# A transformer block on one core: the opening's loads and its order on the engines are changed

## Chip, cores and metric

The kernel runs on one core of a Trainium2 chip, on its five engines: TensorE (PE), VectorE (DVE), ScalarE (ACT), GpSimd (POOL) and SyncE (SP, which issues most DMAs here). The metric is the time of one execution in microseconds (us) on the device; the median of several runs counts.

## What is computed

```python
x = L0_attn_x                                   # (4, 2048, 256)
x = x + layernorm(attn(layernorm(x), Wqk, Wv, Wo, tau))
x = x + layernorm(ffn(layernorm(x), ln_g, ln_b, Wr, W1, W3, W2, W1s, W3s, W2s))

def attn(x):                                    # 16 heads of 16 channels, attention over channels
    qk = heads(x @ Wqk); v = heads(x @ Wv)
    dot = einsum('bhdn,bhen->bhde', qk, qk); q2 = sum(qk * qk, -1)
    logits = (2 * dot - q2[..., :, None] - q2[..., None, :]) / sqrt(n) * tau
    return merge(einsum('bhde,bhen->bhdn', softmax(logits), v)) @ Wo

def ffn(x):                                     # a shared expert and 2 of 7 routed ones, with capacity
    h = layernorm(x) * ln_g + ln_b
    shared = silu(h @ W1s) * (h @ W3s) @ W2s
    return routed(h) + shared
```

## The kernel before

The 8192 rows of x stand in 16 groups of 512 (four tiles of 128 rows each), four groups to a batch. Since the attention mixes channels, a batch needs only the gram matrix of its normalized x (256x256): from it come the scores, the softmax, and one matrix M (Wv, attention and Wo in one) by which all rows of the batch are multiplied. So the program opens with batch 0: load x, normalize its four groups (`x_stats`, `x_norm`), add up the gram on PE (`x_gram`), then the small steps `m_gram` to `m_low` that end in M's high and low half, then per group `o_mix` (x times M), `o_stats`, `o_norm`, `o_apply` (a layernorm, on ScalarE), `o_add` (the residual), `u_stats`, `u_norm` (the second layernorm) and `u_turn0`, `u_turn1` (transposes into h). The feed-forward part then runs in chunks of 512 rows: eight blocks m of products with W1 and W3 (`up`), silu on ScalarE, the product of the two on DVE (L1738), a high and a low half of it (`high`, `low`), and the product with W2 (`down`). Every matmul of large weights is three (`three`, L1140 to L1142): operands are split in a high part and the rest, so each weight piece is copied on ScalarE (`high_piece`, steps `w_first`) and its rest taken on DVE (`low_piece`, steps `w_first_low`); pieces 0 to 3 are W1 and W3, pieces 4 and 5 W2's halves. x transposed is split the same way, by `x_keep` on ScalarE and `x_low` on DVE.

The order is a hand-written table: `put` enters a step, with batch and group, at a place; places -56 to -1 are the opening (`BEFORE` = 56 of them), later ones lie in the chunks, two to a block. Each engine walks the places in turn and issues its own part of every step, so a step's place decides what stands before it in each engine's queue. `attend` does that; in the chunks `between(2 * m)` and `between(2 * m + 1)` call it behind the blocks' own work. `keep_clock` puts products of a matrix of ones behind some steps of the opening, into a bank that nobody reads.

SP issues DMAs in the order of its own list: two groups of x, Wv, the other two, Wqk, and so on. A step `x_stats` has a part on DVE (means and variances) and one on POOL, which raises variances to the power -0.5 (L780, L784, L788). In the first chunk PE's `up` waits for `first_lo` (h's first low half) and `w_lo` (W1's and W3's low parts). A chunk's block m waits until the silu and the product of block m - 1 have read the banks.

## Time and profile before

| | us |
|---|---|
| median of 3 runs (1087.91 to 1089.88) | 1089.29 |
| the profiled execution: its time | 1087.53 |
| its span | 1085.8 |
| PE busy in the span | 1049.2 |
| DVE busy | 656.1 |
| ScalarE busy | 503.5 |
| GpSimd busy | 390.0 |

A time of a run holds the span of the core and what lies around it (here 1.73). The page's busy times are sums over the whole span; PE's 97% is the share in which some matmul was in flight, not the share of its peak. The views that count here show single instructions by time: a row has its start, its length, engine, line and operation, and in brackets the engine's idle time before it and what ended that.

### The profile page before, as it was taken

To read this page: it belongs to the slowest core of one execution; us is meant where nothing else is said; L and a number is where in the kernel's file an instruction comes from. 1 tells how busy PE (TensorE), PEld (TensorE's weight loads), DVE (VectorE), ACT (ScalarE), POOL (GpSimd) and SP (SyncE) were. 2 spreads that over 40 slices of the span, in tenths; PEclk is the share of its full clock that TensorE was granted. 3 is DMA by queue.
4 is the path that set the end of the run, shared out by engine and by line. 5 is a ranking of instruction groups with operands and counts; after the bars stand their busy time and mean duration, and the time that the engine had idled before them with its cause. 6 is when DMAs were issued, how large, how long until landed. Compare 5 with 4: busy or idle time off the path is not lost.

```text
span 1085.8 us, 19513 instructions
## 1 busy us (share of the span) xinstructions
PE 1049.2 (97%) x6863; PEld 958.5 (88%) x6863; DVE 656.1 (60%) x1714; ACT 503.5 (46%) x895; POOL 390.0 (36%) x347
## 2 busy tenths in 40 slices
PE   7998999999999999999989999999999999999995
PEld 6886888888888988889878899999999999999874
DVE  7768864677754578754786334545545463635686
ACT  4343344443434444443454334554546463645485
POOL 3112661114640114541116731344443343312386
PEclk9999999999999999999999999999999999999998
DMA  8322460242540223461134214524344342333699
GB/s 280 114 98 78 138 214 20 78 157 93 174 142 20 100 96 141 134 221 49 59 136 162 93 43 152 139 62 117 82 96 106 68 124 52 81 79 105 239 237 178
DMA packets 47229, 129.15 MB, mean 119 GB/s; under 512 B 10276, under 2 KB 17576, under 8 KB 47152
## 3 DMA queue, kind: packets, MB, share of 16 engines
q1 hardware_dynamic: 28656, 92.83, 25.1%
q0 software_dynamic: 18496, 35.35, 14.2%
q8 instruction: 43, 0.70, 0.3%
q14 instruction: 34, 0.28, 0.1%
HBM read 73.72 MB, written 54.40 MB: 118 GB/s over the span
## 4 chain that ended last, share of the span: by engine, by line
PE 82%; DVE 8%; POOL 3%; issue 3%; ACT 1%; DMA 1%; DVEq 0%; SPq 0%; POOLq 0%; ACTq 0%
PE bank L1140 25%; PE bank L1142 25%; PE bank L1141 25%; PE bank L1159 3%; POOL out_dram L908 2%; POOL sb_place_of L913 2%; DVE sb_act L1738 1%; PE bank L1266 1%; PE bank L1319 1%; DVE sb_act_lo L1714 1%; PE bank L1219 1%; DVE sb_stX L1431 1%; DVE sb_st L1431 1%; PE bank L1278 1%; ACT sb_ln_o L967 1%
## 5 line engine op out<-in xcount | busy, mean ns | idle before, releaser
L1140 PE MATMUL bank<-sb_h_hi,sb_wup_lo 128*128 128x512 f32 (+2 forms) x960 | 354.4, 369 | 5.3 <-DVE sb_act L1738 3.8
L1738 DVE TENSOR_TENSOR sb_act<-bank,sb_act 128x512 f32<-128x512 f32 (+2 forms) x240 | 148.6, 619 | 345.9 <-PE bank L1142 317.1
L1142 PE MATMUL bank<-sb_h_hi,sb_wup_hi 128*128 128x512 f32 (+2 forms) x960 | 350.0, 365 | 0.0
L1141 PE MATMUL bank<-sb_h_lo,sb_wup_hi 128*128 128x512 f32 (+2 forms) x960 | 349.6, 364 | 0.0
L1063 ACT ACTIVATE sb_act<-bank 128x512 f32<-128x512 f32 (+2 forms) x240 | 129.8, 541 | 354.6 <-PE bank L1142 328.9
L1140 PE MATMUL bank<-sb_wdn_hi,sb_act_lo 128*128 128x256 f32 (+1 forms) x848 | 246.5, 291 | 5.8 <-DVE sb_act_lo L1714 5.8
L1142 PE MATMUL bank<-sb_wdn_hi,sb_act_hi 128*128 128x256 f32 (+1 forms) x848 | 240.1, 283 | 0.0
L1141 PE MATMUL bank<-sb_wdn_lo,sb_act_hi 128*128 128x256 f32 (+1 forms) x848 | 239.9, 283 | 0.0
L1140 PEld LDWEIGHTS bank<-sb_h_hi,sb_wup_lo 128*128 128x128 f32 x960 | 180.5, 188 | 27.2 <-DVE sb_act L1738 6.4
L1142 PEld LDWEIGHTS bank<-sb_h_hi,sb_wup_hi 128*128 128x128 f32 x960 | 180.5, 188 | 22.5
L1141 PEld LDWEIGHTS bank<-sb_h_lo,sb_wup_hi 128*128 128x128 f32 x960 | 180.9, 188 | 17.0
L1140 PEld LDWEIGHTS bank<-sb_wdn_hi,sb_act_lo 128*128 128x128 f32 (+1 forms) x848 | 159.7, 188 | 11.6 <-DVE sb_act_lo L1714 6.9
L1714 DVE TENSOR_TENSOR sb_act_lo<-sb_act,sb_act_hi 128x512 fp32r<-128x512 f32 (+2 forms) x240 | 147.2, 613 | 36.1 <-ACT sb_act_hi L1034 34.8
L1141 PEld LDWEIGHTS bank<-sb_wdn_lo,sb_act_hi 128*128 128x128 f32 (+1 forms) x848 | 159.6, 188 | 3.3
L1142 PEld LDWEIGHTS bank<-sb_wdn_hi,sb_act_hi 128*128 128x128 f32 (+1 forms) x848 | 159.5, 188 | 0.0
L1034 ACT ACTIVATE sb_act_hi<-sb_act 128x512 fp32r<-128x512 f32 (+2 forms) x240 | 136.6, 569 | 0.3 <-DVE sb_act L1738 0.3
L864 POOL DMA_INDIRECT y_scratch<-sb_ysb,sb_scur x42 | 76.9, 1832 | 154.1 <-ACT sb_ysb L1052 87.8
L784 POOL TENSOR_TENSOR sb_rstdB<-sb_veB,sb_mhalf 128x4 f32<-128x4 f32 x16 | 19.0, 1187 | 218.1 <-DVE sb_veB L1557 218.1
L800 POOL DMA_INDIRECT sent_scratch<-sb_rows,sb_sendto x64 | 70.7, 1104 | 28.9 <-issue 19.9
L833 POOL DMA_INDIRECT sb_rows<-sent_scratch,sb_gcur x42 | 44.6, 1063 | 77.3 <-issue 52.5
L788 POOL TENSOR_TENSOR sb_rstd<-sb_ve,sb_mhalf 128x4 f32<-128x4 f32 x16 | 19.8, 1239 | 77.5 <-DVE sb_ve L1593 77.5
L967 ACT ACTIVATE sb_ln_o<-bank,sb_nbiasB,sb_rstdB 128x256 f32<-128x256 f32 x64 | 30.9, 563 | 27.5 <-DVE sb_nbiasB L1562 27.5
(265 smaller groups left out, 1240.6 us busy)
## 6 DMA issues: line engine op xcount, KB each, us to landing
sb_xin<-in_L_ffn_W_dram SPq DMA_DIRECT2D x28, 512.0 KB, 3.5
sb_x<-in_L_attn_x_dram SPq DMA_DIRECT2D x16, 512.0 KB, 3.7
out_dram<-sb_x SPq DMA_DIRECT2D x16, 512.0 KB, 3.5
sb_xin<-in_L_attn_x_dram SPq DMA_DIRECT2D x14, 512.0 KB, 5.1
sb_xin<-in_x_turned_dram SPq DMA_DIRECT2D x14, 512.0 KB, 3.9
y_scratch<-sb_ysb SPq DMA_DIRECT2D x14, 512.0 KB, 3.6
sb_xn<-in_L_ffn_W_dram SPq DMA_DIRECT2D x14, 512.0 KB, 3.9
hT_scratch<-sb_hr SPq DMA_DIRECT2D x12, 512.0 KB
```

Source lines behind the costliest of these rows:

```text
L800: pool.indirect_dma_start(sent_d, bass.IndirectOffsetOnAxis(ap=sendto[:, q, t, c:c + 1], axis=0), u[q][:, t, :], None).then_inc(sent[q], 16)
L833: pool.indirect_dma_start(rows[0:w, part, t, :], None, sent_d, bass.IndirectOffsetOnAxis(ap=gcur[0:w, part, t:t + 1], axis=0)).then_inc(ga ...
L864: pool.indirect_dma_start(y_d, bass.IndirectOffsetOnAxis(ap=scur[0:w, par, part, t:t + 1], axis=0), ysb[0:w, part, t, :], None, compute_op ...
L967: ins = s.activation(ln_o[:, t, :], bank[o_bank(b, q) + t // 2][:, (t % 2) * D:(t % 2 + 1) * D], ACT.Identity, scale=rstdB[:, t:t + 1], bi ...
L1034: s.activation(act_hi[:, m % 4, 0:c.w], act[:, m % 3, 0:c.w], ACT.Copy).then_inc(ahi_ok, 1)
L1063: s.activation(act[:, m % 3, 0:c.w], a[:, 0:c.w], ACT.Silu).then_inc(silu_ok, 1)
L1140: t_.matmul(o, a_lo, b_hi, start=start, stop=False, skip_group_check=True)
L1141: t_.matmul(o, a_hi, b_lo, start=False, stop=False, skip_group_check=True)
L1142: return t_.matmul(o, a_hi, b_hi, start=False, stop=stop, skip_group_check=True)
L1159: ins = t_.matmul(bank[4 + k][:, o:c], a[:, k * P:(k + 1) * P], a[:, o:c], start=(q == 0 and t == 0), stop=(q == GB - 1 and t == GT - 1))
L1714: v.tensor_tensor(act_lo[:, m % 4, 0:c.w], act[:, m % 3, 0:c.w], act_hi[:, m % 4, 0:c.w].bitcast(F32), ALU.subtract).then_inc(alo_ok, 1)
L1738: v.tensor_tensor(act[:, m % 3, 0:c.w], bank[(4 if c.wide and m % 2 else 0) + 1][:, 0:c.w], act[:, m % 3, 0:c.w], ALU.mult).then_inc(act_o ...
```

## The change

- SP loads x's four groups first, the first in two halves of two tiles. Then it waits until the third group has landed, and goes on: x transposed (group 0), Wqk, W1's first half, x transposed (group 1), Wv (now to a place of its own, `wv`), Wo, the rest.
- In the four groups of batch 0 DVE normalizes two tiles and writes -mean/deviation (`nbX`), ScalarE normalizes the other two. POOL takes the first power ahead of three of its constants.
- PE begins with 88 products of ones. Wv's transposed product (`wv_turn`) moves from the front to two places behind the attention scores, its copy (`wv_keep`) behind the exponential. Of the ones behind `m_dots`, `m_rowdiag` and `u_turn1` (18, 40, 36), 12 stay behind the second half of `wv_turn` and 12 behind `u_turn1`.
- The table moves `x_keep`, `x_low`, `w_first`, `w_first_low` and `scale_taus`. Two of DVE's steps, W2's second low half and `x_low` of group 3, go into the first chunk.
- The first up-product of the program (`first_up`) starts from the high half of h alone and adds the products with the low half last; ScalarE writes both high halves straight from PSUM.

```diff
         X_FIRST_AT = (("x_stats", (8, 9, 11, 13)), ("x_norm", (10, 12, 14, 15)), ("x_gram", (10, 12, 14, 15)),
-                      ("x_turned", (14, 14, 14, 15)), ("x_keep", (16, 18, 24, 26)), ("x_low", (19, 20, 34, 34)))
+                      ("x_turned", (14, 14, 14, 15)), ("x_keep", (13, 18, 27, 29)), ("x_low", (17, 24, 35, BEFORE + 4)))
         M_FIRST_AT = (20, 22, 22, 23, 24, 25, 26, 28, 30, 31, 32, 33, 34, 35, 36, 36, 37)
...
-        put(0, -BEFORE, 0, [("scale_taus", 25)])
-        for j, at in enumerate((17, 19, 19, 29, 33, 34)):
+        put(0, -BEFORE, 0, [("scale_taus", 23), ("wv_keep", 33)])
+        put(0, -BEFORE, 0, [("wv_turn", 27)])
+        put(0, -BEFORE, 1, [("wv_turn", 31)])
+        for j, at in enumerate((17, 21, 26, 28, 37, 37)):
             put(0, -BEFORE, j, [("w_first", at)])
-        for j, at in enumerate((19, 24, 24, 34, 38, 38)):
+        for j, at in enumerate((19, 24, 34, 45, 49, BEFORE + 2)):
             put(0, -BEFORE, j, [("w_first_low", at)])
...
+            for landed, tiles in ((x_early, slice(0, GT // 2)), (xres_in[0], slice(GT // 2, GT))):
+                sp.dma_start(x2[:, 0, tiles, :], x_t[0][:, tiles, :]).then_inc(landed, 16)
+            sp.dma_start(x2[:, 1, :, :], x_t[1]).then_inc(xres_in[1], 16)
             for k in range(2):
-                sp.dma_start(x2[:, k, :, :], x_t[k]).then_inc(xres_in[k], 16)
+                sp.dma_start(xin[:, k, :, :], x_t[2 + k]).then_inc(x_in_s[k], 16)
...
             for k in range(2):
                 sp.sem_inc(x_in_s[k], 16)
-            weight(tsb, Wv, wv_in)
-            for k in range(2):
-                sp.dma_start(xin[:, k, :, :], x_t[2 + k]).then_inc(x_in_s[k], 16)
+            sp.wait_ge(x_in_s[0], 32)
+            sp.sem_inc(sp_go, 1)
+            turned = lambda q: sp.dma_start(turned_at(0, q).rearrange("p k n -> p (k n)"), x_turned[q]).then_inc(xT_in[q], 16)
+            turned(0)
             weight(wqk, Wqk, const_in)
             w_load(0, 0)
-            for q in range(2):
-                sp.dma_start(turned_at(0, q).rearrange("p k n -> p (k n)"), x_turned[q]).then_inc(xT_in[q], 16)
+            turned(1)
+            weight(wv, Wv, wv_in)
             weight(wo, Wo, const_in)
             for j in (1, 2):
                 w_load(0, j)
...
             made(v.affine_select(out=earlier[:, :], in_=onesb[:, :], compare_op=ALU.is_ge, fill=0.0, base=-1,
                                  pattern=[[1, P]], channel_multiplier=-1))
+            x_rstd(0, 0)
             made(v.affine_select(out=center, in_=center, compare_op=ALU.is_equal, fill=-1.0 / D, base=0,
                                  pattern=[[P, KC], [-1, D]], channel_multiplier=1))
...
+            def x_norm(b, q):
+
+                if b > 0:
+                    return
+                act_e.wait_ge(x_nb, q + 1)
+                x = x2[:, q, :, :] if q < 2 else xin[:, q % 2, :, :]
+                for t, done in ((2, xn_third), (3, xn_ok)):
+                    s.activation(xnorm[q % 2][:, t, :], x[:, t, :], ACT.Identity, scale=rstdX[:, q, t:t + 1],
+                                 bias=nbX[:, q % 2, t:t + 1]).then_inc(done, 1)
...
+            def first_keep(k):
+                act_e.wait_ge(ut_ps, OPEN + k + 1)
+                act_e.wait_ge(vec_in, 48)
+                s.activation(h_hi[:, shared_chunk(0, 0).slot, k, :], bank[6 + k][:, :], ACT.Identity,
+                             scale=gcol[:, k:k + 1], bias=bcol[:, k:k + 1]).then_inc((first_hi, hhi_ok)[k], 1)
+                if k == 1:
+                    s.activation(hfull[:, 1, :], bank[7][:, :], ACT.Identity,
+                                 scale=gcol[:, 1:2], bias=bcol[:, 1:2]).then_inc(hT_ok, 1)
+
             def u_keep(k):
                 def step(b, q):
-                    if opens(b, q) and k == 1:
+                    if opens(b, q):
+                        first_keep(k)
                         return
                     act_e.wait_ge(ut_ps, OPEN + b * (2 * GB) + (2 * q + k + 1))
                     act_e.wait_ge(lg_ps, OPEN + b * GB + q)
-                    if b == 0 and q == 0:
-                        act_e.wait_ge(vec_in, 48)
                     if q == 0:
                         act_e.wait_ge(hlo_ok, b * GB)
                     else:
                         act_e.wait_ge(h_out, OPEN + b * H_LOADS + 16 * (q - 1))
-                    if opens(b, q):
-                        s.activation(h_hi[:, shared_chunk(0, 0).slot, 0, :], bank[6][:, :], ACT.Identity,
-                                     scale=gcol[:, 0:1], bias=bcol[:, 0:1]).then_inc(first_hi, 1)
                     s.activation((hfull if q == 0 else hr)[:, k, :], bank[6 + k][:, :], ACT.Identity,
                                  scale=gcol[:, k:k + 1], bias=bcol[:, k:k + 1]).then_inc(hT_ok, 1)
                 return step
 
-            steps = {"x_high": x_high, "x_keep": x_keep, "m_gram": m_gram,
+            def wv_keep(b, q):
...
-            act_e.wait_ge(wvT_ps, 1)
-            s.activation(wvT[:, :, :].rearrange("p k d -> p (k d)"), bank[6][:, :], ACT.Copy).then_inc(wvT_ok, 1)
             steps["w_first"] = lambda b, j: high_piece(0, j, 0, stage_first)
-            def h_first(b, q):
-                slot = shared_chunk(0, 0).slot
-                act_e.wait_ge(hT_ok, OPEN + 2)
-                s.activation(h_hi[:, slot, 1, :], hfull[:, 1, :], ACT.Copy).then_inc(hhi_ok, 1)
-
             def silu_ready(b, q):
...
-                    if b == 0 and t < GT - 1:
-                        pe.wait_ge(xn_tile, q * (GT - 1) + t + 1)
+                    if b == 0 and t < GT // 2:
+                        pe.wait_ge(xn_tile, q * (GT // 2) + t + 1)
                     elif b == 0:
-                        pe.wait_ge(xn_ok, OPEN + (q + 1))
+                        pe.wait_ge((xn_third, xn_ok)[t - 2], (0, OPEN)[t - 2] + (q + 1))
...
+            def first_up(c):
+
+                pe.wait_ge(first_hi, 1)
+                pe.wait_ge(w_lo, 4)
+                for k, turned in ((0, first_hi), (1, hhi_ok)):
+                    pe.wait_ge(turned, 1)
+                    for which in range(2):
+                        for w in (wup_lo, wup_hi):
+                            t_.matmul(bank[which][:, :], w[c.wset][:, which, k, 0:P], h_hi[:, c.slot, k, :],
+                                      start=(k == 0 and w is wup_lo), stop=False, skip_group_check=True)
+                for k, rest in ((0, first_lo), (1, hlo_ok)):
+                    pe.wait_ge(rest, 1)
+                    for which, full in ((0, a_ps), (1, b_ps)):
+                        ins = t_.matmul(bank[which][:, :], wup_hi[c.wset][:, which, k, 0:P], h_lo[:, c.slot, k, :],
+                                        start=False, stop=(k == KC - 1), skip_group_check=True)
+                        if k == KC - 1:
+                            ins.then_inc(full, 1)
+
...
             def up(c, m, first_wide):
-                opening = isinstance(c.n, int) and c.n == 0 and m == 0
-                if opening:
-                    pe.wait_ge(first_lo, 1)
-                    pe.wait_ge(w_lo, 4)
-                elif m == 0:
+                if isinstance(c.n, int) and c.n == 0 and m == 0:
+                    first_up(c)
+                    return
+                if m == 0:
...
-            pe.wait_ge(const_ok, NCONST)
-            pe.wait_ge(wv_in, 16)
-            for k in range(KC):
+            ONES_MADE = 4
+            pe.wait_ge(const_ok, ONES_MADE)
+            for _ in range(88):
+                t_.matmul(bank[0][:, 0:P], onesb[:, :], onesb[:, :], start=True, stop=True)
+            def wv_turn(b, k):
+                if k == 0:
+                    pe.wait_ge(wv_in, 16)
                 for c in range(KC):
-                    ins = t_.matmul(bank[6][:, k * D:(k + 1) * D], tsb[:, c, k * P:(k + 1) * P], center[:, c, :],
+                    ins = t_.matmul(bank[1][:, k * D:(k + 1) * D], wv[:, c, k * P:(k + 1) * P], center[:, c, :],
                                     start=(c == 0), stop=(c == KC - 1))
-            ins.then_inc(wvT_ps, 1)
+                ins.then_inc(wvT_ps, 1)
+
+            steps["wv_turn"] = wv_turn
             def keep_clock(step, n):
 
                 def paced(b, q):
...
-            for name, n in (("m_times_wqk", {(0, 0): 3}), ("m_dots", {(0, 0): 18}), ("m_rowdiag", {(0, 0): 40}),
+            for name, n in (("m_times_wqk", {(0, 0): 3}), ("wv_turn", {(0, 1): 12}),
                             ("m_times_wo", {(0, 0): 3}), ("m_times_wv", {(0, 0): 6}), ("o_mix", {(0, 1): 25, (0, 2): 35}),
-                            ("u_turn1", {(0, 0): 36})):
+                            ("u_turn1", {(0, 0): 12})):
                 opening_steps[name] = keep_clock(steps[name], n)
...
-                for t in range(GT):
+                for t in range(GT if b > 0 else GT // 2):
                     ins = v.tensor_scalar(xnorm[q % 2][:, t, :], x_from(b, q)[:, t, :], mvX[:, q % 2, t, 0:1],
-                                          rstdX[:, q % 2, t:t + 1],
+                                          rstdX[:, q, t:t + 1],
                                           ALU.subtract, ALU.mult)
-                    if b == 0 and t < GT - 1:
+                    if b == 0:
                         ins.then_inc(xn_tile, 1)
-                ins.then_inc(xn_ok, 1)
+                if b == 0:
+                    v.scalar_tensor_tensor(out=nbX[:, q % 2, :], in0=mvX[:, q % 2, :, 0], scalar=-1.0,
+                                           in1=rstdX[:, q, :], op0=ALU.mult, op1=ALU.mult).then_inc(x_nb, 1)
+                else:
+                    ins.then_inc(xn_ok, 1)
...
             def first_keep(b, q):
                 if opens(b, q):
-                    dve.wait_ge(ut_ps, OPEN + 2)
+                    dve.wait_ge(first_hi, 1)
                     dve.wait_ge(vec_in, 48)
-                    v.tensor_scalar(hfull[:, 1, :], bank[7][:, :], gcol[:, 1:2], bcol[:, 1:2],
-                                    ALU.mult, ALU.add).then_inc(hT_ok, 1)
+                    v.tensor_scalar(hfull[:, 0, :], bank[6][:, :], gcol[:, 0:1], bcol[:, 0:1],
+                                    ALU.mult, ALU.add).then_inc(first_full, 1)
+                    dve.wait_ge(first_full, 1)
+                    dve.sem_inc(hT_ok, 1)
...
             def h_first(b, q):
                 slot = shared_chunk(0, 0).slot
-                dve.wait_ge(hT_ok, OPEN + 2)
                 for k, (ready, done) in enumerate(((first_hi, first_lo), (hhi_ok, hlo_ok))):
+                    if k == 1:
+                        dve.wait_ge(hT_ok, OPEN + 2)
                     dve.wait_ge(ready, 1)
                     v.tensor_tensor(h_lo[:, slot, k, :], hfull[:, k, :], h_hi[:, slot, k, :].bitcast(F32),
...
```

On DVE, between the gram and the scores, before: `sb_u` holds the gram (the copies out of the bank), `sb_wup_lo<-sb_rows` and `<-sb_ysb` are low parts of W1 and W3, `sb_second` and `sb_taus` belong to `scale_taus`, and `sb_hr<-bank,sb_headmask` is the first step of `m_pick`.

```order
L1470 TENSOR_TENSOR sb_wup_lo<-sb_act,sb_wup_hi 128x2x512 [waits xthi_ok]
L1482 COPY sb_u<-bank 128x128 [waits g_done]
L1495 COPY sb_u<-bank 128x128 [waits m_pe,m_chain]
L1695 TENSOR_TENSOR sb_wup_lo<-sb_rows,sb_wup_hi 128x1024 [waits w_hi]
L1695 TENSOR_TENSOR sb_wup_lo<-sb_ysb,sb_wup_hi 128x1024 [waits w_hi]
L1757 TENSOR_REDUCE sb_second<-sb_ident 128x16 [waits tau_in,const_ok]
L1758 TENSOR_SCALAR sb_taus<-sb_taus 128x2
```

The same place in the change (lines are those of the new file):

```order
L1536 COPY sb_u<-bank 128x128 [waits g_done]
L1549 COPY sb_u<-bank 128x128 [waits m_pe,m_chain]
L1813 TENSOR_REDUCE sb_second<-sb_ident 128x16 [waits tau_in,const_ok]
L1814 TENSOR_SCALAR sb_taus<-sb_taus 128x2
L1524 TENSOR_TENSOR sb_wup_lo<-sb_act,sb_wup_hi 128x2x512 [waits xthi_ok,tau_ok]
L1751 TENSOR_TENSOR sb_wup_lo<-sb_rows,sb_wup_hi 128x1024 [waits w_hi]
L1560 TENSOR_TENSOR sb_hr<-bank,sb_headmask 128x256 [waits m_pe,h_out,lg_ps]
```

`scale_taus`, with its wait for tau, now comes first behind the gram's copies, and `x_low` of group 1 (L1524) moved from before them to behind them.

On DVE in the first chunk, from block 1's product (`sb_act<-bank,sb_act`) to the next group's second norm, before (`sb_lg` are the router's values, `sb_st` and `sb_mv` statistics of `u_stats`):

```order
L1738 TENSOR_TENSOR sb_act<-bank,sb_act 128x512 [waits b_ps,silu_ok]
L1628 STREAM_TRANSPOSE sb_lg<-bank 128x128 [waits lg_ps]
L1714 TENSOR_TENSOR sb_act_lo<-sb_act,sb_act_hi 128x512 [waits dn_done,ahi_ok]
L1431 BN_STATS sb_st<-sb_x 128x6 [waits x2_ok]
L1431 BN_STATS sb_st<-sb_x 128x6 x3
L1435 BN_AGGR sb_mv<-sb_st 128x2 [waits u_chain]
L1435 BN_AGGR sb_mv<-sb_st 128x2 x3
L1593 TENSOR_SCALAR sb_ve<-sb_mv 128x4 [waits u_chain]
L1738 TENSOR_TENSOR sb_act<-bank,sb_act 128x512 [waits b_ps,silu_ok]
L1714 TENSOR_TENSOR sb_act_lo<-sb_act,sb_act_hi 128x512 [waits dn_done,ahi_ok]
L1608 TENSOR_SCALAR sb_rows<-sb_x,sb_mv,sb_rstd 128x256 [waits w_lo,b_rstd2]
```

And in the change:

```order
L1794 TENSOR_TENSOR sb_act<-bank,sb_act 128x512 [waits b_ps,silu_ok]
L1751 TENSOR_TENSOR sb_wdn_lo<-sb_ysb,sb_wdn_hi 128x1024 [waits w_hi]
L1684 STREAM_TRANSPOSE sb_lg<-bank 128x128 [waits lg_ps]
L1770 TENSOR_TENSOR sb_act_lo<-sb_act,sb_act_hi 128x512 [waits dn_done,ahi_ok]
L1476 BN_STATS sb_st<-sb_x 128x6 [waits x2_ok]
L1476 BN_STATS sb_st<-sb_x 128x6 x3
L1480 BN_AGGR sb_mv<-sb_st 128x2 [waits u_chain]
L1480 BN_AGGR sb_mv<-sb_st 128x2 x3
L1647 TENSOR_SCALAR sb_ve<-sb_mv 128x4 [waits u_chain]
L1794 TENSOR_TENSOR sb_act<-bank,sb_act 128x512 [waits b_ps,silu_ok]
L1524 TENSOR_TENSOR sb_wup_lo<-sb_xin,sb_wup_hi 128x2x512 [waits xthi_ok]
L1770 TENSOR_TENSOR sb_act_lo<-sb_act,sb_act_hi 128x512 [waits dn_done,ahi_ok]
```

W2's second low half (L1751) stands behind the product of block 1 and ahead of the statistics, `x_low` of group 3 (L1524) behind the product of block 2.

## Rows read from the trace of the kernel before

**Rows 1.** The page: PE's clock by fortieths of the span; the chain's shares by engine.

```profile
PEclk9999999999999999999999999999999999999998
...
PE 82%; DVE 8%; POOL 3%; issue 3%; ACT 1%; DMA 1%; DVEq 0%; SPq 0%; POOLq 0%; ACTq 0%
```

**Rows 2.** PE's waits, whole span: waiting line, engine waited for, us in total, times, longest.

```profile
PE bank L1140 <- DVE sb_act L1738: 3.8, 4, 2.8
...
PE bank L1140 <- ACT sb_act L1063: 1.3, 1, 1.3
```

**Rows 3.** PE's timeline: start, length, line, operation, count, idle before and its end.

```profile
6.64 3.75 PE L1382 MATMUL bank<-sb_ysb,sb_u 128*128 128x256 f32 x8 [6.64 <-DMA sb_u<-in_L_attn_Wv_dram]
10.19 3.89 PE L1159 MATMUL bank<-sb_xn 128*128 128x256 f32 x16
13.91 2.78 PE L1159 MATMUL bank<-sb_ln_o 128*128 128x256 f32 x16
16.53 2.78 PE L1159 MATMUL bank<-sb_xn 128*128 128x256 f32 x16
```

**Rows 4.** DVE's timeline while x is normalized.

```profile
4.50 1.40 DVE L1431 BATCH_NORM_STATS2 sb_stX<-sb_x 128x6 f32<-128x256 f32 x4 [4.50 <-DMA sb_x<-in_L_attn_x_dram]
...
8.59 1.38 DVE L1460 TENSOR_SCALAR sb_xn<-sb_x,sb_mvX,sb_rstdX 128x256 f32<-128x256 f32 x4
...
11.93 1.38 DVE L1460 TENSOR_SCALAR sb_ln_o<-sb_x,sb_mvX,sb_rstdX 128x256 f32<-128x256 f32 x4
```

**Rows 5.** DMA issues: destination, source, count, KB each, us from issue to landing.

```profile
sb_u<-in_L_attn_Wv_dram SPq DMA_DIRECT2D x1, 256.0 KB, 3.1
...
sb_taus<-in_L_attn_tau_dram SPq DMA_DIRECT2D x2, 0.1 KB, 4.5
```

**Rows 6.** POOL's timeline: the constant of ones, and the first power.

```profile
1.07 0.21 POOL L744 MEMSET sb_onesb<- 128x128 bf16 x1
...
6.71 1.03 POOL L780 TENSOR_TENSOR sb_rstdX<-sb_veX,sb_mhalf 128x4 f32<-128x4 f32 x1 [0.41 <-DVE sb_veX L1449]
```

**Rows 7.** ScalarE's timeline at the start of the first chunk.

```profile
48.51 0.78 ACT L986 ACTIVATE sb_h_hi<-bank,sb_bcol,sb_gcol 128x512 fp32r<-128x512 f32 x1 [5.88 <-PE bank L1250]
...
54.72 1.93 ACT L967 ACTIVATE sb_ln_o<-bank,sb_nbiasB,sb_rstdB 128x256 f32<-128x256 f32 x4 [1.68 <-DVE sb_nbiasB L1562]
56.53 0.61 ACT L1063 ACTIVATE sb_act<-bank 128x512 f32<-128x512 f32 x1
```

**Rows 8.** PE's timeline: the ones behind u_turn1.

```profile
48.53 2.17 PE L1390 MATMUL bank<-sb_onesb 128*128 128x128 bf16 x36
```

**Rows 9.** DVE's timeline: the first step of m_pick.

```profile
25.80 0.42 DVE L1506 TENSOR_TENSOR sb_hr<-bank,sb_headmask 128x256 f32<-128x256 f32 x1
```

**Rows 10.** SP's timeline: the issue of tau.

```profile
11.51 4.31 SPq L669 DMA_DIRECT2D sb_taus<-in_L_attn_tau_dram  x8
```

**Rows 11.** The chain that ended last, in order of time: start, length, what.

```profile
25.49 5.23 DMA sb_ysb<-in_L_ffn_W2s_dram
30.75 1.06 ACT sb_wdn_hi L1028
...
35.07 2.27 DVE sb_wdn_lo L1695 x2
```

**Rows 12.** DVE's timeline: h's low halves, and the product of block 2.

```profile
49.99 1.35 DVE L1767 TENSOR_TENSOR sb_h_lo<-sb_hfull,sb_h_hi 128x512 fp32r<-128x512 f32 x2 [0.45 <-ACT sb_hfull L988]
...
61.26 0.69 DVE L1738 TENSOR_TENSOR sb_act<-bank,sb_act 128x512 f32<-128x512 f32 x1
```

**Rows 13.** PE's timeline: block 2's start, and its wait in block 3.

```profile
57.21 0.48 PE L1140 MATMUL bank<-sb_h_hi,sb_wup_lo 128*128 128x512 f32 x1
...
62.00 0.50 PE L1140 MATMUL bank<-sb_h_hi,sb_wup_lo 128*128 128x512 f32 x1 [0.36 <-DVE sb_act L1738]
```

**Rows 14.** Stretches: length; busy (count) of PE, PEld, DVE, ACT, POOL; clock, DMA share, GB/s.

```profile
108.00:110.00 2.00, 2.00 (x6) 1.55 (x5) 1.64 (x6) 0.00 (x0) 0.00 (x0) 0.50 0.00 0
110.00:112.00 2.00, 2.00 (x13) 1.96 (x12) 2.00 (x8) 0.00 (x0) 1.48 (x2) 0.64 0.01 4
```

38 lines of the change are left out of this document (24 added, 14 removed).

## The prediction

> **What bounds the kernel now.** Times are us from the start of the span. I read the chain that ended last, PE's waits, the timelines of the opening engine by engine, and the DMA issues. In the chain PE holds 82% [rows 1]. So a change of the opening is worth as much as PE's work in the first shared chunk comes earlier, if nothing takes it back before PE runs without holes. After the opening PE waits little: behind DVE's product with the silu 3.8 in the whole run, one of them 2.8, and once 1.3 behind the silu itself [rows 2]. The opening is one chain: PE waits 6.64 for Wv, multiplies it, and the gram follows [rows 3]. A whole group of the gram takes 2.62 (13.91 to 16.53); the first takes 3.72, since PE starts at the lower of its two rates: eight matmuls 128x256 take 3.75 there, 0.47 each, and at that pace a group would take 5.6. (The clock's row of the page shows full rate from the start [rows 1]; the durations do not.) The gram ends at 21.95. DVE stands before it [rows 4]: statistics from 4.50, two groups' statistics before the first normalizing at 8.59, whose four tiles cost 1.38.
>
> After the gram come 13.2 us of small steps up to the mixing (35.1), then the mixing itself, a norm, a sum and a second norm. The last of them, u_norm, ends 47.8; from it the first chunk starts.
>
> **The gram: -2.45.** x's first two tiles are 256 KB; Wv's 256 KB landed 3.1 after issue [rows 5], so they land at 0.81 + 3.1 = 3.9, the others at 4.5 as now. DVE's statistics of group 0 end near 5.95 instead of 6.6. The power, 1.03 long [rows 6], ends at 7.0. DVE goes on with group 1 to 8.0, normalizes, and the first tile is there at 8.4. Per group DVE has 3.35 of work (8.59 to 11.93); two tiles fewer (0.65) and one small product more (0.1) make it 2.8. ScalarE's two tiles cost about 0.5 each, by o_apply's four in 1.93 [rows 7], beside other work; its queue is idle there. PE's 2.62 a group stays the bound, if the higher rate is there from the start.
>
> For that stand the 88 products of ones, from 1.4 (their constant is written at 1.28). At the full rate they take 0.06 each (36 in 2.17, [rows 8]), at the lower twice that. Before, PE ran slow from 6.64 to about 12.3 (the first group takes 1.1 longer, so 2.2 of it is slow), 5.7 in all. Released as late as that, at 7.1, the ones end at 9.4 (47 slow, 41 fast) and the gram at 9.4 + 4 x 2.62 = 19.9; released early enough, they end before the first tile, DVE is the bound up to the third group (its first tile at 13.95), and the gram ends at 19.2. I take 19.5: 2.45 earlier. The Trainium skill (TensorE: Matmul & The Clock Gate, "Part 1: The HAM clock gate") says that the low rate is the state at rest, that activity ends it, and that the moment varies from run to run. The trace agrees on the slow start; by the skill either end may come out, and the sum moves by 0.3.
>
> **From the gram to u_norm: -0.3.** Two things are put before the attention scores' first step (m_pick, 25.80 [rows 9]) on DVE. scale_taus now comes ahead of x_low(1) and W1's second low half; the queue from m_sym on is 0.5 + 1.2 + 1.2, so m_pick starts 4.05 after the gram instead of 3.85: +0.2. And scale_taus needs tau. Its eight loads went out from 11.51 in 4.31 [rows 10], the last at 15.3, and that one landed 4.5 later, at 19.8 [rows 5]. SP now waits for x's third group (landing about 7) before eight loads of about 0.5, so the last tau goes out near 17.0: landed between 20.1, if the same bytes ahead of it decide, and 21.5. DVE wants it at 19.5 + 1.15 = 20.65. So it is 0 to 0.9 late; I take +0.3, nearer the lower end, since the 4.5 was mostly queue. x_turned's last two loads go out behind tau, at 17.4, and are wanted at 23.4: hidden.
>
> W2: before, ScalarE waits for W2's second half (the chain has its DMA for 5.23 and its copy at 30.75 [rows 11]), and the copies of Wo's product, whose first bank is done at 30.9, begin at 31.8. With W2 behind m_high the first begins at once and the second when its bank is done: 0.75 gained. The load has time: ScalarE takes W2's second half about 34 and o_apply comes at 37.9. Wv's product (4 instructions of 0.24 each half) falls into PE's waits, beside m_pick and m_logits (25.80 to 28.9); its copy, 0.6 on ScalarE, lies between exp and Wo: nothing. o_stats, behind two low halves of W2 (2.27 from 35.07 [rows 11]), is then bound by the mixing itself, which ends at 37.85: 0.1. W1's last low half (1.2) before o_add ends when o_add can start: 0.05 lost. So 0.2 + 0.3 - 0.75 - 0.1 + 0.05 = -0.3.
>
> At u_norm's end the lead is 2.45 + 0.3 = 2.75. From here I give times in the frame of before; the lead is taken off at the end.
>
> **The first chunk: +1.6.** Before, the first up-product starts at 50.74, behind the ones and the first low half of h (49.99 on [rows 12]); block 0 is done at 53.65. Now PE needs only the high half (49.3, a copy of 0.78 from 48.51 [rows 7]), and its first block ends at about 52.2: 1.4 won. But block 2 waits for the silu of block 1, and that stands behind o_apply of group 1 on ScalarE: o_apply from 54.72, the silu at 56.53, PE's block 2 at 57.21 [rows 7, 13]. o_apply hangs on the statistics that DVE begins when h's two low halves are done, 1.35 from 49.99 [rows 12]. Those end no earlier now: the full halves come one after another (high 0 to 49.3, high 1 to 50.0, full 1 on ScalarE to 50.7, low 1 on DVE to 51.45). So block 2 starts at 57.4, **+0.2**; the 1.4 becomes a wait of PE.
>
> DVE gets two steps more in the chunk: W2's second low half behind the product of block 1, and x_low(3) behind that of block 2, 1.15 each (two of W2's in 2.27 [rows 11]). The product of block 2 runs at 61.26 [rows 12], and PE already waits for it, 0.36 at 62.00 [rows 13]. The low half in front moves it to 62.6: **+1.15**, all of it PE's. x_low(3) delays u_norm of group 1 and with it the transposes that PE comes to; PE, itself late, meets them 0.25 late: **+0.25**. Behind that DVE has holes, and PE runs without one to 92. SP now holds load, store and residual behind x_low(3) (about 64); the store and the residual load move some 7 and 3, and what needs them comes at 97: hidden.
>
> **Sum.** -2.45 - 0.3 + 1.6 = -1.15. The profiled execution took 1087.53 (span 1085.8); it becomes 1086.4. The three runs have their median 1.76 above it, at 1089.29; so **1088.1**, 0.1% less: within 0.2%, about what a measurement of this kernel can tell from no change.
>
> **The rivals.**
> *The first chunk costs nothing in the end (0.38).* PE waits 2.8 once more, behind DVE, at 104.87 to 107.62 [rows 2]. If that hole gives back what the first chunk lost, the lead of 2.75 stays: 1086.5, faster. For it: DVE has idle time between the chunk and that hole. Against: DVE's row of work before the hole begins at 80.88 with a product for which it waits on PE, so a late PE moves the hole with it. Were the extra steps cheaper in place, the result lies between.
>
> *PE falls back to the lower rate (0.12): slower.* Of the 58 ones behind the scores, 12 are left, and Wv's product does not fill the rest; between m_dots and Wo's product PE stands idle about 2.2 of 5 instead of 1.0, and in the first chunk twice for 1.6. After the hole of 2.75 the granted clock was 0.50 and then 0.64 [rows 14], the 1.2 GHz level, for some 3.4; that costs 2 x 0.5 + 2 x 0.36 = 1.7. In the opening the low rate could last as long as the first time, 5.6, over Wo's and Wv's products and the mixing: 2.8. Both: -1.15 + 2.8 + 1.7 = +3.35, 1092.6. It decides from the point where one such gap counts as rest; against it, the hole of 1.3 [rows 2] left the rate alone. The Trainium skill (same page, "HAM oscillation — how this bites in real kernels") says that pauses between bursts bring the low rate back, to be paid each time; the hole at 107 agrees, and by it this rival would have both falls.
>
> *tau comes at its latest (0.08).* +0.6 on top, 1088.7: still within 0.2%.
>
> **How the numbers follow.** The forecast alone has 0.42. Within 0.2%: 0.42 + 0.08 = 0.50; faster 0.38; slower 0.12. The lower end: gram at 19.2, tau in time, no cost in the first chunk, 2.75 + 0.3 + 0.3 = 3.35 under the median, and 0.95 for the runs' own spread (1087.91 to 1089.88): 1085.0. The upper: gram at 19.9, tau at its latest, -1.15 + 0.4 + 0.6 = -0.15, one fall of the clock of 1.7, and 0.15 for the rounding of the steps: 1091.0. The likeliest case alone spans 1086.9 to 1089.3.
>
> **What would show it.** Right: gram's end at 19.2 to 19.9; m_pick 4 behind it; no W2 on ScalarE before Wo's copies; PE's first up-block 1.4 earlier after u_norm, then a wait for a silu before block 2 and one of about 1.5 for block 2's product. Wrong: matmuls of ones at twice their length up to the gram, any slow stretch between 22 and 70, DVE waiting for tau's DMA by over 1, or a lead at 110 as large as at u_norm.

## The result and the profile after

The change makes the kernel slower: 1089.63 us (median of 20 runs, 1088.10 to 1094.04) against 1087.18 for the kernel before (20 runs, 1084.92 to 1091.51). The ratio on record is 1.0026, 95% interval 1.0015 to 1.0036 (it comes from all the runs, here and below, and so is not quite the quotient of the medians). The forecast was a gain of 1.15 us. One execution of chunk_free, a kernel further down, took 1709.58 at a granted clock of 0.56; it is left out of that kernel's ratio. The profiled execution took 1089.85 (span 1088.1), the one of before 1087.53 (1085.8): 2.3 more.

PE's timeline after the change, in the opening and in the first chunk, answers to [rows 3, 13] (start, length, line, operation, count, idle before and what ended it):

```profile
1.33 6.37 PE L1420 MATMUL bank<-sb_onesb 128*128 128x128 bf16 x88 [1.33 <-POOL sb_onesb L760]
10.19 4.53 PE L1183 MATMUL bank<-sb_xn 128*128 128x256 f32 x16 [2.49 <-DVE sb_xn L1510]
14.55 2.78 PE L1183 MATMUL bank<-sb_ln_o 128*128 128x256 f32 x16
...
19.80 2.78 PE L1183 MATMUL bank<-sb_ln_o 128*128 128x256 f32 x16
...
47.98 0.61 PE L1271 MATMUL bank<-sb_ident,sb_u 128*128 128x128 f32 x4
...
57.77 0.50 PE L1164 MATMUL bank<-sb_h_hi,sb_wup_lo 128*128 128x512 f32 x1 [1.43 <-ACT sb_act L1095]
63.71 0.50 PE L1164 MATMUL bank<-sb_h_hi,sb_wup_lo 128*128 128x512 f32 x1 [1.49 <-DVE sb_act L1794]
66.82 0.66 PE L1290 MATMUL bank<-sb_ident,sb_rows 128*128 128x128 f32 x4
...
74.85 0.65 PE L1302 MATMUL bank<-sb_hr,sb_wr 128*32 128x128 f32 x16
```

The gram starts at 10.19, the very moment at which it started before, though Wv's product no longer stands ahead of it: PE is idle for 2.49 behind the ones, since no normalized tile is there. Then the first group takes 4.36 (10.19 to 14.55), the others 2.62. The gram ends at 22.6; before, at 21.95. Two more of PE's rows of before belong beside this, u_norm's transposes of group 0 and the router's product for group 1:

```profile
47.65 0.61 PE L1247 MATMUL bank<-sb_ident,sb_u 128*128 128x128 f32 x4
...
72.90 0.64 PE L1278 MATMUL bank<-sb_hr,sb_wr 128*32 128x128 f32 x16
```

DVE's timeline, to be held against [rows 4, 12]:

```profile
3.67 1.41 DVE L1476 BATCH_NORM_STATS2 sb_stX<-sb_x 128x6 f32<-128x256 f32 x4 [3.67 <-DMA sb_x<-in_L_attn_x_dram]
...
7.57 1.41 DVE L1476 BATCH_NORM_STATS2 sb_stX<-sb_x 128x6 f32<-128x256 f32 x4 [1.77 <-DMA sb_x<-in_L_attn_x_dram]
...
9.63 0.74 DVE L1510 TENSOR_SCALAR sb_xn<-sb_x,sb_mvX,sb_rstdX 128x256 f32<-128x256 f32 x2
...
59.00 1.21 DVE L1751 TENSOR_TENSOR sb_wdn_lo<-sb_ysb,sb_wdn_hi 128x1024 fp32r<-128x1024 f32 x1
...
62.97 0.69 DVE L1794 TENSOR_TENSOR sb_act<-bank,sb_act 128x512 f32<-128x512 f32 x1
63.58 1.21 DVE L1524 TENSOR_TENSOR sb_wup_lo<-sb_xin,sb_wup_hi 128x1024 fp32r<-128x1024 f32 x1
```

Group 0's first half is there at 3.67, 0.83 before the whole group was there before. But group 1 makes DVE wait 1.77, and the first normalizing, queued behind its statistics, goes from 8.59 to 9.63. The stretches after the change show the loading, and then the clock (columns as in [rows 14]):

```profile
3.00:3.50 0.50, 0.50 (x8) 0.50 (x6) 0.00 (x0) 0.00 (x0) 0.44 (x3) 1.00 1.10 385
3.50:4.00 0.50, 0.50 (x8) 0.50 (x6) 0.33 (x1) 0.00 (x0) 0.50 (x1) 1.00 0.76 197
4.00:4.50 0.50, 0.50 (x11) 0.50 (x10) 0.50 (x3) 0.00 (x0) 0.43 (x4) 1.00 0.71 229
4.50:5.00 0.50, 0.50 (x13) 0.50 (x11) 0.50 (x2) 0.00 (x0) 0.50 (x3) 1.00 0.70 254
...
10.00:11.00 1.00, 0.81 (x5) 0.79 (x6) 1.00 (x5) 0.53 (x2) 0.92 (x1) 0.94 0.68 238
11.00:12.00 1.00, 1.00 (x4) 0.82 (x4) 0.85 (x5) 0.57 (x2) 0.00 (x0) 0.50 0.99 376
12.00:13.00 1.00, 1.00 (x5) 0.91 (x4) 0.97 (x7) 0.00 (x0) 0.44 (x1) 0.50 1.26 325
13.00:14.00 1.00, 1.00 (x5) 0.82 (x4) 1.00 (x5) 0.75 (x2) 0.68 (x1) 0.50 0.57 176
14.00:15.00 1.00, 1.00 (x7) 0.89 (x6) 0.85 (x6) 1.00 (x2) 0.00 (x0) 0.86 0.91 328
```

From 3.5 to 5.0 only 197 to 254 GB/s come in. And the granted clock, 1.00 up to 10, is 0.50 (the 1.2 GHz level) from 11 to 14: the ones had brought the higher rate (8 of them lie in the half microsecond from 3.5, 13 in that from 4.5), the clock fell after the hole behind them, and the gram's first group is again the slow one. So the ones bought nothing in this execution.

From there on the gap to before can be followed at marks that both kernels have: u_norm's transposes of group 0, and the bursts in which PE multiplies by the router's weights. There are sixteen of these, one for each group; "the router" below is the second, that of group 1 (at 74.85 here, 72.90 before), since it lies behind the steps that the change puts into the first chunk. Gram's end +0.6, transposes +0.33 (47.98 to 47.65), router +1.95. The first chunk costs the 1.6. The gap then stays: +2.2 at the router's burst at 547. Behind that it moves with spells of low clock that come at other places: before has one at 568 to 572 (granted 0.70, then 0.50), the changed kernel one at 1050 to 1055 (0.81), and the spans end 2.3 apart.

### The profile page after: what moved, and what is told of

It is laid out like the page before. It is cut to its first block, busy times and chain, and to the rows that moved or that the text cites. A ratio compares the mean times of both kernels' runs of the same rounds, so it can differ in the third digit from the quotient of the medians.

```text
span 1088.1 us, 19555 instructions
## 1 busy us (share of the span) xinstructions
PE 1050.9 (97%) x6881; PEld 960.1 (88%) x6881; DVE 654.6 (60%) x1710; ACT 508.1 (47%) x903; POOL 386.3 (36%) x347
## 4 chain that ended last, share of the span: by engine, by line
PE 81%; DVE 10%; POOL 4%; issue 3%; ACT 1%; DMA 1%; DVEq 0%; POOLq 0%; SPq 0%; ACTq 0%
PE bank L1164 25%; PE bank L1166 24%; PE bank L1165 24%; PE bank L1183 3%; POOL out_dram L921 2%; POOL sb_place_of L926 2%; DVE sb_act L1794 1%; DVE sb_act_lo L1770 1%; PE bank L1343 1%; PE bank L1290 1%; DVE sb_stX L1476 1%; DVE sb_st L1476 1%; ACT sb_ln_o L990 1%; PE bank L1243 1%; PE bank L1213 1%
## 5 line engine op out<-in xcount | busy, mean ns | idle before, releaser
L1164 PEld LDWEIGHTS bank<-sb_wdn_hi,sb_act_lo 128*128 128x128 f32 (+1 forms) x848 | 159.5, 188 | 10.5 <-DVE sb_act_lo L1770 5.8
L813 POOL DMA_INDIRECT sent_scratch<-sb_u,sb_sendto x32 | 36.2, 1131 | 19.4 <-DVEq L1739 11.0
```

Source lines behind the costliest of these rows:

```text
L813: pool.indirect_dma_start(sent_d, bass.IndirectOffsetOnAxis(ap=sendto[:, q, t, c:c + 1], axis=0), u[q][:, t, :], None).then_inc(sent[q], 16)
L1164: t_.matmul(o, a_lo, b_hi, start=start, stop=False, skip_group_check=True)
```

## The experiments

For every run: gram's end, u_norm's transposes of group 0, and the router burst of group 1 (us from the start of the span); then the gap to before at the burst that before has at 547.3; then the ratio to before with its 95% interval.

| kernel | gram | transposes | router | at 547 | ratio |
|---|---|---|---|---|---|
| before | 21.95 | 47.65 | 72.90 | 0 | 1 |
| after | 22.6 | 47.98 | 74.85 | +2.2 | 1.0026 (1.0015 to 1.0036) |
| ones_130 | 22.1 | 48.20 | 75.06 | +2.3 | 1.0024 (1.0014 to 1.0034) |
| xin_later | 20.1 | 48.66 | 75.51 | +2.7 | 1.0023 (1.0009 to 1.0037) |
| no_split | 20.1 | 46.21 | 73.09 | +0.4 | 1.0000 (0.9990 to 1.0010) |
| lows_open | 20.8 | 48.15 | 73.63 | +0.7 | 1.0017 (1.0007 to 1.0028) |
| tau_back | 20.3 | 45.60 | 72.47 | -0.4 | 1.0004 (0.9995 to 1.0013) |
| chunk_free | 20.0 | 46.08 | 71.58 | +0.3 | 0.9998 (0.9989 to 1.0008) |
| both | 20.1 | 45.46 | 70.97 | -1.6 | 0.9990 (0.9981 to 1.0000) |
| no_ones | 21.5 | 46.91 | 73.78 | +1.0 | 1.0010 (1.0001 to 1.0019) |
| split_rows | 21.4 | 47.47 | 74.32 | +1.6 | 1.0027 (1.0017 to 1.0036) |
| old_up | 20.3 | 45.63 | 71.18 | -1.5 | 0.9989 (0.9979 to 0.9999) |
| dve_norm | 21.4 | 46.47 | 71.95 | -1.0 | 0.9996 (0.9986 to 1.0006) |
| shadow | 20.1 | 46.34 | 71.83 | -0.8 | one run, 1088.04 |

Each kernel has one trace. Six kernels have the same program up to the gram (no_split, tau_back, chunk_free, both, old_up, shadow), and their gram ends between 20.0 and 20.3: so much a mark can differ with nothing changed ahead of it, and by 1.8 where the clock falls in one and not in the other (after, lows_open). The intervals of the ratios reach about 1 us to either side, so the marks carry most verdicts. My theory at first: group 1 of x lands late because two more groups share the engines with it, the clock fell in the hole, and the chunk cost what was forecast. The rivals: the split loads do it; the tiles, not the clock, make the first group slow; a later hole gives the chunk back.

**ones_130.**

```diff
-            for _ in range(88):
+            for _ in range(130):
```

> The changed kernel with 130 products of ones ahead of the gram instead of 88; nothing else differs. Theory (the clock fell in the hole behind the ones): the 42 more, 0.058 each, fill the 2.49 that PE stands idle from 7.70 to 10.19; the granted clock then stays at 1.00 over the gram, the gram's first group takes 2.6 instead of 4.4, the gram ends near 20.8 instead of 22.6, and the time falls by 1.2 to 1.8 (less if tau, whose loads are not moved, comes late). Rival (the first group is slow because its tiles come slowly): the ones end at 10.2, the first group still takes over 4, the time does not move.

```profile
1.33 10.24 PE L1420 MATMUL bank<-sb_onesb 128*128 128x128 bf16 x130 [1.33 <-POOL sb_onesb L760]
11.41 2.84 PE L1183 MATMUL bank<-sb_xn 128*128 128x256 f32 x16
14.08 2.78 PE L1183 MATMUL bank<-sb_ln_o 128*128 128x256 f32 x16
```

PE's timeline: no hole, and the first group takes 2.67. So the slow group of the change was the clock, not its tiles (lows_open, below, shows the same without more ones). But the ones end at 11.4, not at 10.2, and now they hold the gram: it ends 0.5 earlier, not 1.8, and nothing of it reaches u_norm (DVE waits 0.64 for tau instead). The higher rate comes at another moment each time; the same 88 ones took 6.37 after the change, 7.17 in no_split, 7.94 in xin_later.

**xin_later.** The loads of groups 2 and 3 go behind SP's increments.

```diff
             sp.dma_start(x2[:, 1, :, :], x_t[1]).then_inc(xres_in[1], 16)
-            for k in range(2):
-                sp.dma_start(xin[:, k, :, :], x_t[2 + k]).then_inc(x_in_s[k], 16)
...
                 sp.sem_inc(x_in_s[k], 16)
+            for k in range(2):
+                sp.dma_start(xin[:, k, :, :], x_t[2 + k]).then_inc(x_in_s[k], 16)
             sp.wait_ge(x_in_s[0], 32)
```

> The changed kernel with the loads of x's third and fourth groups issued behind SyncE's increments, where the kernel before has them, instead of straight behind x's second group. Theory (the second group's transfer shares the DMA engines with the two behind it): x's second group lands near 5.7 instead of 7.5, the first normalized tile is there at 8.5, PE stands idle under 1 behind the ones, the clock stays, the gram ends at 19.0 to 20.0 instead of 22.6, and the time falls by 2 to 3.5, to 0.1 to 0.3 per cent under the changed kernel. Rival (the half loads with their rows of 2 KB, or their later issue, are what holds it): the second group still lands past 7 and nothing moves.

Group 1 landed at 6.57 (DVE waits 0.43 for it) and the gram ended at 20.1. So the two loads behind it do take part of the bandwidth: without them between 2.2 and 3.9, the two halves and group 1 come in at over 300 GB/s.

```profile
3.50:4.00 0.50, 0.50 (x8) 0.50 (x6) 0.01 (x1) 0.00 (x0) 0.50 (x1) 1.00 1.33 315
4.00:4.50 0.50, 0.50 (x7) 0.50 (x6) 0.50 (x2) 0.00 (x0) 0.43 (x4) 1.00 0.83 336
4.50:5.00 0.50, 0.50 (x7) 0.50 (x6) 0.50 (x2) 0.00 (x0) 0.50 (x3) 1.00 0.97 311
```

But u_norm came later than in any other kernel, and the time did not fall. PE's timeline, and the stretches:

```profile
26.41 0.41 PE L1228 MATMUL bank<-sb_hr,sb_headmask 128*128 128x32 f32 x2 [1.68 <-DVE sb_hr L1564]
...
29.59 2.08 PE L1234 MATMUL bank<-sb_wvo,sb_hr 128*128 128x256 f32 x4 [0.72 <-DVE sb_hr L1592]
...
31.78 3.38 PE L1243 MATMUL bank<-sb_u,sb_wvo 128*128 128x256 f32 x8
```

```profile
28.00:30.00 2.00, 1.28 (x10) 1.02 (x8) 1.63 (x7) 0.71 (x2) 0.00 (x0) 0.50 0.04 16
30.00:32.00 2.00, 2.00 (x8) 1.46 (x8) 1.80 (x2) 0.68 (x2) 0.00 (x0) 0.50 0.22 31
32.00:34.00 2.00, 2.00 (x5) 1.57 (x6) 0.00 (x0) 0.25 (x2) 0.00 (x0) 0.50 0.80 229
```

The four products with Wo take 2.08 instead of 1.13, at a clock of 0.50: the fall of the forecast's second rival, at its place, in the stretch whose 58 ones were cut to 12. From the gram's end to the transposes it costs 2.4 against no_split, whose gram ends at the same time (48.66 to 46.21); the rival had been priced at 2.8 for that stretch. In the change itself and in the eleven other runs the clock held there (1.13 for the same products), with holes of 0.6 to 1.6 in front of the row's diagonal; here the hole is 1.68. No run puts the 58 ones back, so that their absence did it is not shown, and why the clock fell in this execution and not in no_split (hole 1.59) stays open.

**no_split.**

```diff
-            for landed, tiles in ((x_early, slice(0, GT // 2)), (xres_in[0], slice(GT // 2, GT))):
-                sp.dma_start(x2[:, 0, tiles, :], x_t[0][:, tiles, :]).then_inc(landed, 16)
+            sp.dma_start(x2[:, 0, :, :], x_t[0]).then_inc(xres_in[0], 16)
```

> The changed kernel with x's first group in one load of 512 KB, as before the change, the other loads as in the change. Theory (sharing with the third and fourth groups): the second group of x still lands at 7 or later, the first statistics start at 4.3 or later instead of 3.67, the gram's end moves by less than 0.6 either way. Rival (the halves are what holds the second group): it lands at 6 or before, the first tile is there at 8.5, and the gram ends 2 earlier.

My theory (that the two loads behind do it alone) falls, the rival holds. (DVE's waits follow the edit: it waits for the whole group.) DVE's timeline and the stretches:

```profile
4.47 1.40 DVE L1475 BATCH_NORM_STATS2 sb_stX<-sb_x 128x6 f32<-128x256 f32 x4 [4.47 <-DMA sb_x<-in_L_attn_x_dram]
...
6.52 1.40 DVE L1475 BATCH_NORM_STATS2 sb_stX<-sb_x 128x6 f32<-128x256 f32 x4
...
22.20 0.37 DVE L1809 TENSOR_REDUCE sb_second<-sb_ident 128x16 f32<-128x128 f32 x1 [0.90 <-DMA sb_taus<-in_L_attn_tau_dram]
```

```profile
3.50:4.00 0.50, 0.50 (x8) 0.50 (x6) 0.00 (x0) 0.00 (x0) 0.50 (x1) 1.00 1.02 385
4.00:4.50 0.50, 0.50 (x7) 0.50 (x6) 0.03 (x1) 0.00 (x0) 0.43 (x4) 1.00 0.98 401
4.50:5.00 0.50, 0.50 (x7) 0.50 (x6) 0.50 (x2) 0.00 (x0) 0.50 (x3) 1.00 1.06 434
```

With one load of 512 KB the same bytes come in at 385 to 434 GB/s where the two halves left 197 to 254. Group 0 is complete 0.8 after the first half had been, and group 1 is there in time, though the same two loads stand behind it. By its issue and its landing time group 1 lands at 5.7, against 7.5 after the change and 6.5 in xin_later. SP gets past its wait for group 2 at 7.08 instead of 8.91, and the gram ends at 20.1, 2.5 earlier; undoing this one edit brings the time back to that of before. So the late landing needs both, the halves and two more groups right behind: take away either, and the gram ends at 20.1. What is left of the gain is eaten behind it: tau, now wanted before it lands, holds DVE for 0.90 at 22.20, and the chunk costs 1.6 as in the change.

**lows_open.**

```diff
-                      ... ("x_low", (17, 24, 35, BEFORE + 4)))
+                      ... ("x_low", (17, 24, 35, 40)))
-        for j, at in enumerate((19, 24, 34, 45, 49, BEFORE + 2)):
+        for j, at in enumerate((19, 24, 34, 44, 45, 49)):
```

> The changed kernel with VectorE's three late low halves moved into holes of the opening: that of x_turned's last group behind the mixing's m_low (hole of 1.42 at 35.4), W1's last one ahead of the norm of group 0 (hole of 1.12 at 39.7), W2's first behind it and W2's second at 48.2, so that none is left in the first chunk. Theory (the chunk loses 1.15 + 0.25 to the two steps in it, and nothing gives it back later): block 2's product comes at 61.9 or before instead of 62.97, PE's wait for it is 0.3 instead of 1.49, group 1's transposes come 1.2 to 1.5 earlier than 66.82, and the whole time falls by 1.2 to 1.5. Rival (the hole of 2.8 near 108 takes back what the chunk gives): the transposes move and the whole time stays within 0.4. Second rival: the moved steps delay u_norm (46.85) by as much as the chunk gains.

The gram, which this edit does not touch, ended at 20.8 and not at 22.6:

```profile
9.84 2.86 PE L1183 MATMUL bank<-sb_xn 128*128 128x256 f32 x16 [1.87 <-DVE sb_xn L1510]
12.53 2.87 PE L1183 MATMUL bank<-sb_ln_o 128*128 128x256 f32 x16
```

Group 1 was late here too (DVE waits 1.25 for it and starts at 7.22), but the hole behind the ones was 1.87, the clock held, and the first group took 2.69. So of the change's 22.6 the late landing is in every trace with these loads, and the slow first group only in that of the change itself. Transposes to router took 25.48 instead of 26.87: the chunk gives back 1.4. But the norm of group 0 lost 0.9: POOL's power took 1.92 instead of 1.01, with W1's low half on DVE beside it. The second rival, in part; tau_back, chunk_free and shadow take it apart.

**tau_back** (on no_split).

```diff
-        put(0, -BEFORE, 0, [("scale_taus", 23), ("wv_keep", 33)])
+        put(0, -BEFORE, 0, [("scale_taus", 25), ("wv_keep", 33)])
```

> The changed kernel with x's first group in one load (as in no_split), and tau's scaling on VectorE put back behind the two low halves that the change put behind it. Theory (tau's landing at 22.2 holds VectorE for 0.90 in no_split, with the two low halves of 1.14 each queued behind the wait): the wait goes, the scores' first step starts at 24.1 instead of 24.96, PE's wait in front of the row's diagonal falls from 1.6 to 0.7, u_norm's transposes come 0.9 earlier than 46.21, and the time falls by 0.7 to 0.9 against no_split. Rival (ScalarE's queue of high halves, late W3, is next): the exponential waits for a W1 or W3 half, and under 0.4 is left.

DVE's wait for tau is gone, and PE's wait ahead of the row's diagonal fell from 1.59 to 0.85. The transposes come 0.6 earlier with a gram that ended 0.16 later: 0.77 in place of 0.9. The ratios do not show it (1.0004 and 1.0000, with overlapping intervals), so the mark alone carries this.

**chunk_free** (on no_split).

```diff
-                      ... ("x_low", (17, 24, 35, BEFORE + 4)))
+                      ... ("x_low", (17, 24, 35, 40)))
-        for j, at in enumerate((19, 24, 34, 45, 49, BEFORE + 2)):
+        for j, at in enumerate((19, 24, 34, 45, 49, BEFORE + 1)):
```

> The changed kernel with x's first group in one load, with the low half of x_turned's last group in the hole ahead of group 0's statistics (1.42 at 35.4 in the changed kernel), and W2's second low half in the hole of 2.0 in which VectorE waits for o_apply of group 1 (55.25 to 57.26 there). Neither runs beside a power of GpSimd. Theory (the two steps in the chunk cost 1.4 and nothing gives it back): PE's wait for block 2's product falls from 1.49 to 0.4 or less, group 1's transposes come 1.2 to 1.5 earlier than 65.05, and the time falls by 1.1 to 1.5 against no_split, to 0.05 to 0.2 per cent under the kernel before. Rival (a hole further on gives it back): the transposes move by that, the time by under 0.5.

PE's wait for block 2's product fell from 1.49 to 0.37; group 1's transposes came at 63.62 instead of 65.05, the router 1.51 earlier. At the mark before has at 96 the 1.3 against before is still there; behind it, in this one execution, the clock falls for longer than in the others (granted 0.78 over 100 to 110), and the gap is 0.0 at the next burst. The ratio lies 0.02% under before, less than expected, with an interval that does not exclude the 0.1%.

**both** (the edits of tau_back and chunk_free on no_split).

> The edits of tau_back and of chunk_free together, on the changed kernel with x's first group in one load. Theory (the two add up): u_norm's transposes 0.9 earlier and group 1's 2.1 to 2.4 earlier than in no_split, and the time 1.8 to 2.4 under it, some 0.15 to 0.25 per cent under the kernel before. Rival (the hole near 108 or a fall of the clock takes part of it): under 1.

PE's timeline of the first chunk, to be held against that of after:

```profile
55.24 0.51 PE L1163 MATMUL bank<-sb_h_hi,sb_wup_lo 128*128 128x512 f32 x1 [1.41 <-ACT sb_act L1094]
60.06 0.50 PE L1163 MATMUL bank<-sb_h_hi,sb_wup_lo 128*128 128x512 f32 x1 [0.37 <-DVE sb_act L1790]
63.01 0.60 PE L1289 MATMUL bank<-sb_ident,sb_rows 128*128 128x128 f32 x4
```

The two add up: router 2.12 earlier than in no_split, 1.93 earlier than before, and 1.6 of it still there at 547. The ratio gives 0.10% under before, 1.1 us, less than the 1.8 to 2.4 that were expected, and the interval just reaches 1. The chunk now costs 0.26 (lead 2.19 at the transposes, 1.93 at the router).

**no_ones** (on no_split). The 88 ones are left out; they compute nothing that is read.

> The changed kernel with x's first group in one load and without the 88 products of ones. Theory (at the start PE is at its lower rate until it has worked for a while): the gram's first two groups run with matmuls of 0.33 spacing instead of 0.16, the gram ends at 22 to 23 instead of 20.1, and the time is up by 1.5 to 2.5 against no_split. Rival (the clock is up anyway by 9): the gram ends within 0.5 of 20.1.

```profile
9.09 4.55 PE L1182 MATMUL bank<-sb_xn 128*128 128x256 f32 x16 [9.09 <-DVE sb_xn L1504]
13.47 2.78 PE L1182 MATMUL bank<-sb_ln_o 128*128 128x256 f32 x16
```

One group runs slow, not two: the gram ends at 21.5, earlier than expected. So the ones are worth 1.4 at the gram's end when only a short hole follows them (0.62 in no_split), and 0.7 at the router, since with the later gram tau is hardly waited for.

**split_rows.** The two loads of group 0 again, but cut by partitions, with rows of 4 KB as in a whole load.

```diff
-            for landed, tiles in ((x_early, slice(0, GT // 2)), (xres_in[0], slice(GT // 2, GT))):
-                sp.dma_start(x2[:, 0, tiles, :], x_t[0][:, tiles, :]).then_inc(landed, 16)
+            for landed, rows in ((x_early, slice(0, P // 2)), (xres_in[0], slice(P // 2, P))):
+                sp.dma_start(x2[rows, 0, :, :], x_t[0][rows, :, :]).then_inc(landed, 16)
...
                     dve.wait_ge(x_early, 16)
+                    dve.wait_ge(xres_in[0], 16)
```

> The changed kernel with x's first group still in two loads, but cut by partitions (64 each, with rows of 4 KB) instead of by tiles (128 partitions with rows of 2 KB); VectorE's statistics of that group wait for both. Theory A (the short rows are what slows the loading): the transfer rate shows no drop under 300 GB/s between 3 and 7.5, x's second group is there before VectorE wants it (its statistics start without a wait, near 6.6), SyncE gets past its wait by 7.6, and the gram ends near 20.3. Theory B (one more load ahead of it, issued 0.48 later, is what delays it): the second group lands past 7 and SyncE gets past its wait after 8.3, as in the changed kernel.

```profile
4.50:5.00 0.50, 0.50 (x8) 0.50 (x6) 0.00 (x0) 0.00 (x0) 0.50 (x3) 1.00 0.35 82
5.00:5.50 0.50, 0.50 (x8) 0.50 (x6) 0.00 (x0) 0.00 (x0) 0.02 (x1) 1.00 1.23 205
```

The drop is there with rows of 4 KB too, and deeper; SP gets past its wait at 9.07. So the length of the rows is not what makes it (that a load to 64 partitions is slow for a reason of its own is not excluded). Theory B holds: the loading ends late, and group 1, issued at 2.08, lands 5.6 later, at 7.7, as its row among the DMA issues says (DVE comes to it at 7.79 only, so its timeline can't show that):

```profile
sb_x<-in_L_attn_x_dram SPq DMA_DIRECT2D x1, 512.0 KB, 5.6
```

Why two loads at the head of the queue slow what follows by more than their second issue (0.48), when two more groups stand right behind, stays open.

**old_up** (on both). PE's first block waits for h's low halves again, behind 36 ones.

```diff
-                if isinstance(c.n, int) and c.n == 0 and m == 0:
-                    first_up(c)
-                    return
-                if m == 0:
+                opening = isinstance(c.n, int) and c.n == 0 and m == 0
+                if opening:
+                    pe.wait_ge(first_lo, 1)
+                    pe.wait_ge(w_lo, 4)
+                elif m == 0:
...
                     for k in range(KC):
+                        if opening and k == 1:
+                            pe.wait_ge(hlo_ok, 1)
...
-                            ("u_turn1", {(0, 0): 12})):
+                            ("u_turn1", {(0, 0): 36})):
```

> The kernel of both with the first block of up-products back in the order of before (it waits for h's low halves) and with the 36 ones ahead of it. Theory (block 2 is held by the silu behind o_apply, so an earlier block 0 only waits): block 0 starts 1.3 to 1.7 later, PE's wait of 1.41 behind the silu shrinks to under 0.3, block 2 starts at most 0.6 later than 55.24, and the time moves by at most 0.6 against both. Rival (the earlier block is what makes both fast): block 2 and all behind it come 1.3 or more later.

Block 0 starts at 49.01 instead of 47.25, PE's wait for the silu is gone, and block 2 starts at 55.49 instead of 55.24, of which 0.2 is the gram's later end. The router is 0.21 later, the ratio the same. The earlier first block is worth nothing, as forecast.

**dve_norm** (on both).

```diff
-                if b > 0:
-                    return
+                return
                 act_e.wait_ge(x_nb, q + 1)
...
-                for t in range(GT if b > 0 else GT // 2):
+                for t in range(GT):
...
-                        ins.then_inc(xn_tile, 1)
-                if b == 0:
-                    v.scalar_tensor_tensor(out=nbX[:, q % 2, :], ...).then_inc(x_nb, 1)
-                else:
+                        ins.then_inc((xn_tile, xn_tile, xn_third, xn_ok)[t], 1)
+                if b > 0:
                     ins.then_inc(xn_ok, 1)
```

> The kernel of both with all four tiles of a group normalized on VectorE, as before the change, and none on ScalarE. Theory (with the loads in order PE's 2.62 a group is the bound, and VectorE's 3.35 a group would take its place): the groups of the gram start over 3 apart, PE waits for normalized tiles by 0.4 to 1.2 in all, and the gram ends 0.5 to 1.2 later than 20.1; the time is up by as much. Rival (VectorE has slack enough): the gram ends within 0.3 of 20.1.

```profile
9.26 2.86 PE L1181 MATMUL bank<-sb_xn 128*128 128x256 f32 x16 [0.60 <-DVE sb_xn L1505]
12.53 2.88 PE L1181 MATMUL bank<-sb_ln_o 128*128 128x256 f32 x16 [0.41 <-DVE sb_ln_o L1505]
15.87 2.88 PE L1181 MATMUL bank<-sb_xn 128*128 128x256 f32 x16 [0.46 <-DVE sb_xn L1505]
```

Groups come 3.3 apart, and PE waits for DVE at two of them: the gram ends 1.3 later, the router comes 1.0 later. So ScalarE's two tiles are worth about 1.1 once PE is fast and x there (0.16 of the 1.3 is x's later landing).

**shadow** (on both). W1's last low half goes from behind the norm's bias to ahead of it, as in lows_open.

```diff
-        for j, at in enumerate((19, 24, 34, 45, 49, BEFORE + 1)):
+        for j, at in enumerate((19, 24, 34, 44, 49, BEFORE + 1)):
```

> The kernel of both with one step moved: W1's last low half on VectorE goes ahead of the norm's bias of group 0 instead of behind it, into the time in which VectorE waits for GpSimd's power. Theory (a subtraction of two tiles on VectorE and GpSimd's power exclude each other, as in lows_open, where the power took 1.92 instead of 1.01): the power of group 0 takes 1.8 to 2.0, and u_norm's transposes come 0.7 to 1.0 later than 45.46 after the gram's end is taken off. Rival (the 1.92 was chance): it takes 1.0 to 1.3 and the transposes move by 0.2 or less.

POOL's timeline with that step moved, and then that of both:

```profile
37.22 1.92 POOL L796 TENSOR_TENSOR sb_rstdB<-sb_veB,sb_mhalf 128x4 f32<-128x4 f32 x1 [21.85 <-DVE sb_veB L1607]
```

```profile
37.26 1.01 POOL L796 TENSOR_TENSOR sb_rstdB<-sb_veB,sb_mhalf 128x4 f32<-128x4 f32 x1 [21.87 <-DVE sb_veB L1607]
```

One step moved into an idle stretch of DVE, and the power takes 0.91 longer; the transposes come 0.88 later. The theory fits: the power took 1.92 in both kernels with this step there, and 1.01 in the twelve others.

## Why the prediction was wrong

**The step that failed is the gram's term, -2.45, and in it the sentence "DVE goes on with group 1 to 8.0", which takes group 1 of x to land as before.** In the profiled execution the term measured +0.6. From 19.5 the forecast's gram would start at 19.5 - 4 x 2.62 = 9.0; it started at 10.19, 1.2 later, because the halves, with groups 2 and 3 right behind, slowed x's loading and group 1 came at 7.57. The first group took 4.36 instead of 2.62, 1.7 more, because the clock fell after the hole so made. 1.2 + 1.7 and 0.2, for which the last group ends later than 2.62 after its start (2.78), are the 3.1 between 19.5 and 22.6. The late start is in every trace with these loads; the 1.7 is not: in lows_open the clock held, and the term was -1.15, about half of the forecast. I had taken the landing of a 256-KB load from Wv's row and left group 1 where it was; no row of before shows two half loads at the head of the queue, and I gave this unknown a single value where it needed two ends. The Trainium skill (SBUF — State Buffer, "The DMA setup-cost knee") advises to coalesce into the largest single transfer. The run no_split agrees (the gram ends at 20.1 with one load, 22.6 with two), and weighed against the change the advice would have been a rival; xin_later shows two halves without that cost (20.1), when the next loads are issued later.

Of the clock I had put the fall between the scores and the mixing, not before the gram. The change shows it before the gram, xin_later at the forecast's place. One reading was off without a place in the sum: at 0.47 for each matmul a group of sixteen takes 7.5, not 5.6.

The measured 1089.63 lies inside the stated 1085.0 to 1091.0, but by luck: the three runs of before that the forecast started from have their median 2.1 above that of the 20 runs.

**The two other terms came out, one of them in part by luck.** From the gram's end to u_norm the forecast was -0.3; from +0.64 to +0.33 it is -0.3. Its parts came out too, for the most part: m_pick starts 4.2 behind the gram instead of 3.85 (+0.3, forecast 0.5 for queue and tau), no W2 stands before Wo's copies, and from m_pick to the mixing 0.66 is gained. But tau cost nothing here only because the gram was late. With the gram at 20.1 (no_split) DVE waits 0.90 for it, 0.3 in the forecast, and the term is +0.4: the last of tau's loads goes out at 18.5 there, not near 17.0. The chunk was +1.6 and is +1.62 (1.95 - 0.33); chunk_free takes out the 1.4 of the two steps, and the 0.26 left in both is about the 0.2 of o_apply. That the earlier block 0 becomes a wait of PE: 1.43 in the profile, and old_up shows it.

**The rivals.** That a later hole gives the chunk back is refuted: the 1.95 at group 1's router burst is 2.2 at 547, and both keeps its 1.9 as 1.6. With x loaded in one piece the forecast's -1.15 would have failed too, if by less. The run no_split has -1.85 for the gram (its four groups take 11.0, not 10.5: DVE needs 2.8 for each, 8.57 to 11.36), +0.4 up to u_norm (tau's 0.9 in it), +1.6: about +0.2, and it measures 1.0000.

## What to carry to other kernels

A transfer cut in two so that its first half comes sooner can delay what is queued right behind it: read the rate of the stretch, not only the landing of the piece. Work that only keeps PE's clock up is worth what its gap to the real work leaves: ones that end 2.5 early lost their gain, ones that end 1.9 early kept it, and 42 more of them held the gram. A step put into an engine's idle stretch is free only if the wait that makes the stretch does not need what the step uses, and in a chain the slot that is truly free (here before o_apply's sum) is worth looking for.

## What the runs showed of the hardware

- Two half loads at the head of the queue and two more groups right behind: 82 to 254 GB/s for 1 us or more (after, ones_130, lows_open; split_rows), with rows of 2 KB as of 4 KB. One whole load gave 385 to 434 (no_split), two halves with the next loads issued 1.7 later 303 to 344 (xin_later).
- DVE's subtraction of two tiles (1.22) lengthened POOL's power from 1.01 to 1.92, twice. The Trainium skill (SBUF — State Buffer, "Who interferes with whom") says that a VectorE instruction with two inputs in SBUF contends with a GpSimd instruction that reads SBUF; the trace agrees, by 0.91.
- The moment at which PE's rate rises varied: 88 products took 6.37 to 7.94. A fall followed holes of 2.49 (after) and 1.68 (xin_later), none followed 1.87 (lows_open). Of the fourteen traces eleven show a fall after the hole of 2.75 to 2.77 near 107, three (lows_open, tau_back, dve_norm) none.
